# Order of two VectorE operations in the fifth step of each FFN chunk, in a macaron block on one core

## The reference, cut to what matters

```python
gate = jnp.einsum('bsd,hd->bsh', x, wg)      # x: layer norm of the input, 256 -> 768
up = jnp.einsum('bsd,hd->bsh', x, wu)
h = jax.nn.silu(gate) * up
ffn = jnp.einsum('bsh,dh->bsd', h, wd)       # 768 -> 256
x = x + 0.5 * ffn(layernorm(x))
x = x + attn(layernorm(x))                   # causal, 16 heads
x = x + 0.5 * ffn(layernorm(x))
```

## Time and profile before

| | |
|---|---|
| runs before | 1781.88 to 1790.09 us, median 1786.74 us |
| the profiled execution | 1802.57 us, of which 1800.8 us from the first to the last instruction |
| TensorE busy | 1630.5 us (91%), mean granted clock 0.942 |
| VectorE busy | 1206.3 us (67%) |
| ScalarE busy | 1024.0 us (57%) |
| GpSimd busy | 427.6 us (24%) |

### The profile page before, as it was taken

How to read it: one execution, slowest core, us unless ns; L and a number is a source line. 1 busy time by engine, 2 the same in 40 slices (tenths; PEclk the granted TensorE clock), 3 DMA queues, 4 the chain that set the end, 5 groups by cost and what they waited for, 6 DMA issues and landing times. The chain is left out here.

```text
span 1800.8 us, 37764 instructions
## 1 busy us (share of the span) xinstructions
PE 1630.5 (91%) x12418; PEld 942.9 (52%) x12418; DVE 1206.3 (67%) x2701; ACT 1024.0 (57%) x2032; POOL 427.6 (24%) x656
## 2 busy tenths in 40 slices
PE   5999999459999989989989989989998887999998
PEld 4888888314444334334334334334343236888887
DVE  5565654378888878778878768777877725655553
ACT  4444443137767757657757757757766655434343
POOL 3454544311101101101101011111010003544443
PEclk9999999659999989889989989989999898999999
DMA  7000000400200200100200200200200001101011
GB/s 240 1 0 0 0 0 1 139 13 18 61 14 21 58 14 21 58 14 8 71 14 8 63 19 11 58 20 11 62 22 11 5 1 54 36 23 35 23 35 36
DMA packets 46949, 58.46 MB, mean 32 GB/s; under 512 B 6112, under 2 KB 33504, under 8 KB 46816
## 3 DMA queue, kind: packets, MB, share of 16 engines
q1 hardware_dynamic: 46816, 56.51, 10.2%
HBM read 30.53 MB, written 25.17 MB: 31 GB/s over the span
## 5 line engine op out<-in xcount | busy, mean ns | idle before, releaser
L1045 ACT ACTIVATE at_probs<-at_banks 128x512 f32<-128x512 f32 (+1 forms) x1280 | 635.7, 560 | 350.2 <-PE at_banks L1233 269.2
L1149 DVE TENSOR_REDUCE at_maxima<-at_banks 128x1 f32<-128x512 f32 (+3 forms) x1024 | 532.7, 581 | 162.9 <-PE at_banks L1233 121.2
L1225 PE MATMUL at_banks<-at_q_rows,at_k_rows 30*128 30x512 bf16 (+3 forms) x1536 | 322.2, 343 | 62.8 <-issue 33.3
L1225 PE MATMUL at_banks<-at_k_rows,at_q_rows 27*128 27x512 bf16 (+3 forms) x1536 | 331.5, 348 | 25.7 <-DMA at_q_rows<-q_rows_dram 16.2
L1252 PE MATMUL at_o_ps<-at_probs,at_v_aug 128*32 128x512 f32 (+3 forms) x3072 | 338.3, 530 | 8.7 <-ACT at_probs L1045 5.6
L390 PE MATMUL ffn_gate_up<-ffn_x_hi,ffn_w_hi 128*128 128x512 f32 x768 | 307.5, 400 | 19.5 <-DVE ffn_x_lo L274 11.8
L181 POOL TENSOR_TENSOR ffn_h_lo<-ffn_h_sb,ffn_h_hi 128x512 fp32r<-128x512 f32 x192 | 247.2, 1295 | 261.1 <-ACT ffn_h_hi L210 223.5
L390 PE MATMUL ffn_gate_up<-ffn_x_lo,ffn_w_hi 128*128 128x512 f32 x768 | 304.1, 396 | 0.0
L291 DVE TENSOR_TENSOR ffn_h_sb<-ffn_act_sb,ffn_gate_up 128x512 f32<-128x512 f32 x192 | 131.5, 686 | 237.4 <-PE ffn_gate_up L390 135.2
L217 ACT ACTIVATE ffn_act_sb<-ffn_gate_up 128x512 f32<-128x512 f32 x192 | 115.1, 600 | 308.0 <-PE ffn_gate_up L390 302.7
L1225 PEld LDWEIGHTS at_banks<-at_q_rows,at_k_rows 30*128 30x128 bf16 x1536 | 83.9, 92 | 379.7 <-issue 134.3
(11 more groups left out here) (84 smaller groups left out, 1490.4 us busy)
## 6 DMA issues: line engine op xcount, KB each, us to landing
x<-x_in SPq DMA_DIRECT2D x16, 512.0 KB, 4.6
at_k_rows<-k_rows_dram SPq DMA_DIRECT2D x32, 256.0 KB, 2.8
at_q_rows<-q_rows_dram SPq DMA_DIRECT2D x64, 128.0 KB, 2.1
out<-x SPq DMA_DIRECT2D x16, 512.0 KB, 2.9
q_rows_dram<-at_qk_parts SPq DMA_DIRECT2D x72, 96.0 KB, 2.4
k_rows_dram<-at_qk_parts SPq DMA_DIRECT2D x72, 96.0 KB, 2.4
at_q_rows<-at_max_t SPq DMA_DIRECT2D x256, 3.0 KB
ffn_w_f<-w_gate SPq DMA_DIRECT2D x2, 768.0 KB, 5.2
```

The costliest lines, as they stand in the source:

```text
L1045: nc.scalar.activation(probs[:, (g * NE + u) % PROBS, j, 0:n], banks[:, used[0], 0:n], ACT.Exp).then_inc(exp_done, 1)
L1149: last = nc.vector.tensor_reduce(out, banks[:, used[0], o:o + n], AX_X, ALU.max)
L1225: last = nc.tensor.matmul(banks[:, n, o:o + width], stationary, moving, start=(k == 0), stop=(k == len(pieces) - 1 and not masks))
```

## The change

In step 4 VectorE subtracts the two halves of `x_lo` first and adds the second half of the residual behind them. In step 3 nothing changes.

```diff
--- before.py
+++ after.py
@@ -301,10 +301,10 @@
                 up(m)
                 if m == 0 and not last:
                     ln_gather()
+                if m == 4 and not last:
+                    split_x(c + 1, 1 - p)
                 if m in (3, 4) and not first:
                     residual(c - 1, m - 3)
-                if m == 4 and not last:
-                    split_x(c + 1, 1 - p)
 
         ln_stats(0, 0)
         dve.wait_ge(stats_done, 1)
```

## The result

The changed kernel took 1768.61 us (median of 8 runs, 1761.36 to 1776.30) and the kernel before, in the same sessions, 1788.41 us (8 runs, 1776.65 to 1795.90). The ratio is 0.9893 with a 95% interval of 0.9862 to 0.9925: 13 to 25 us less, 19.8 us by the medians. The forecast was 15.9 us less and 1770.8 us. The profiled execution after is the slowest of the eight (1776.30 us), and the one before, 1802.57 us, is slower than all eight, so times are compared by the medians and the traces only stretch by stretch.

What follows compares the result with a forecast made beforehand. TensorE bounds the FFN stages, stopping for `x_lo` at 28 chunk boundaries; 11.0 + 2.1 + 2.8 = 15.9 us off the median of 1786.74 gives 1770.8 us, range from 5.8 us below that to 1779.0.

Steps and rivals of the forecast that it cites:

- The bound and the stop: FFN stages: TensorE sets the pace; its stop for `x_lo` at chunk boundaries, 0.51 us in ffn1, goes wholly.
- `x_lo` at its new place: VectorE, directly behind `up(4)`: the pair still takes about 1.28 us and is good 0.6 us ahead of TensorE's load.
- The slow restart: TensorE behind each boundary stop: second matmul after 0.33 instead of 0.23 us; 28 x 0.10 = 2.8 us gained.
- The residual and `up(5)`: VectorE, step 4 to 5: the later residual costs nothing and `up(5)` keeps its time, with 0.5 us of cover.
- GpSimd as the next to be late: First `down` of a chunk: `h_lo` holds with 0.24 us of cover; rival that it fails, about 1775 us, chance 0.08.
- The sum: 28 FFN chunk boundaries: 11.0 us in the loop, 2.1 outside it, 2.8 of slow restarts, together 15.9 us.
- the loop edge: FFN loop-head jumps: their delay takes the wait's place at 14 boundaries, 8.0 us left of the gain, 1778.7 us; chance 0.12.
- the clock in attention: Attention stage: TensorE's granted clock falls, 11.6 us more per hundredth, making the kernel slower, about 1795 us; chance 0.05.
- a change of attention by more than some 5 us: Attention stage: its length changing by more than some 5 us was set as a sign that the prediction is wrong.

Runs made afterwards that it cites:

- the last kernel: Changed kernel, attention included, with the last chunk's first `down` waiting for `h_lo` part by part: 1768.33 us (7 runs), ratio 0.9893 to the kernel before.

## Why the prediction was right

The measured 1768.61 us lie 2.2 us below the forecast. That they lie so near is in part luck: the forecast went out from a median of 1786.74 us of three runs, where eight gave 1788.41. By the difference it was 15.9 us against 19.8, of which about 17 belong to the FFN stages.

- **The bound and the stop.** Right. TensorE's order is the same, the stops of rows 4 and 9 are gone, and the forecast's 0.61 us a chunk was 0.62 in ffn1 and 0.63 in ffn2.
- **`x_lo` at its new place.** Right: 1.29 us for the pair, beside ScalarE and GpSimd. The text gave it 0.6 us of cover with the signal counted; measured are 0.80 to the load, 0.67 with the signal. The reason was tested apart: one extra subtraction is free, two are not.
- **The slow restart.** Right as a cost of its own: it vanished with the stop, came back with a stop of 0.30 us, and appeared without any stop when `h_lo` came at the last moment. The rows of the load say why: released late, it goes out with its matmul (142.92 and 142.93) instead of 0.23 us ahead, and costs 0.10 us; with 0.10 us of lead (140.57 and 140.67) it costs 0.01.
- **The residual and `up(5)`.** Right: `up(5)` starts 0.49 us after the step's last matmul starts (141.02 to 141.51), before it was 0.53, and one step later the addition costs nothing either.
- **GpSimd as the next to be late.** Right that it is the nearest and that it holds; the 0.24 us with the signal were measured as 0.23. But the text took the operand load as the deadline, and `x_lo` 0.14 us behind it cost only 0.03 us a chunk. By the matmul's own time the cover is 0.46 us.
- **The sum.** A little low: 15.9 us forecast, 16.9 in the traces of the whole kernel, 17.3 without attention. In the trace before, the 28 stops add up to 13.3 us and the slow restarts to 2.9, 16.2 in all, so the count was 0.3 us low. Of that 0.1 us are the three boundaries a stage outside the loop, taken as the middle of two rows (0.35 us each; in the trace they are 0.39, 0.43 and 0.31 in ffn1 and 0.37, 0.42 and 0.30 in ffn2). The other 0.7 us is spacing of the matmuls that differs by fractions of a percent between the executions, and was not settled.
- **The rivals: the loop edge.** It costs nothing: 0.23 us at each jump. The text said that no row shows a jump by itself; there is one, in the trace before too, with 0.21 to 0.24 us, and the sequencer makes the jump some 3 us before the boundary's first matmul. The rule of the Trainium skill that spoke for the rival (Runtime: NRT & Kernel Launch, Instruction fetch mechanics) is about a target outside the instruction window. The trace agrees with it: the attention loop's jumps move instruction packets and take 3.6 to 4.3 us, and the FFN loop's, during which none moves, are not such a case. So the text applied the rule to the wrong loop. That the attention loop is the longer one (some 1130 matmuls an iteration against 208) fits, but no run here changed a loop's length.
- **The rivals: the clock in attention.** It did move, in the friendly direction, 9.5 us in the profiled execution. The text named a change of attention by more than some 5 us as a sign that the prediction is wrong. That sign came, and it was badly set: attention differs by 18.3 us between the traces of the new order and of the last kernel, and the kernel before scatters as much by itself. The price was 11.6 us for each hundredth of clock, and the three stretches give somewhat less, 27.8 us for the 0.03 from 0.91 to 0.94. Which way it moves is chance as far as these runs show, which is why the kernels without attention were needed to measure 17 us well.

## What to carry to other kernels

On an engine that works in order, look at what stands in front of the instruction that the bounding engine waits for: if that one waits for something nobody needs soon, exchange the two, and count the stop from start to start with the slow restart behind it (0.51 + 0.10 us here, against 0.34 us of idle time in the waits). Then compute what is late next against the new, earlier time, to the matmul's start and not only to its operand load, and check the cover with extra work whose length is read from a trace in which it stands where it will stand: here it was free up to the threshold, and past it cost its lateness and the slow restart. Look at the rows of the sequencer before a jump is blamed. Where a stage without changes scatters more than the gain, leave it out for the measurement.

## What the runs showed of the hardware

- An operand that became good between the time of a matmul's operand load and the matmul's own time delayed almost nothing at first: 0.14 us behind the load cost 0.03 us a chunk (the residual between the halves), 0.23 us cost 0.10 (three additions on GpSimd). After a late release the second matmul started 0.33 us after the first with 512 columns and 0.22 with 256, where an unbroken stream has 0.23 and 0.12.
- After a stop of 3.3 us at a stage's end the next 48 matmuls ran at a granted clock of 1.00 at six stage ends and lower at seven, 5.4 to 5.7 against 7.1 to 8.3 us. The kernel whose stop was split into two of 1.0 to 1.3 us scattered by 0.5 us over four runs, the others by 1.5 to 4.3.
- A jump of TensorE's sequencer to the head of the FFN loop took 0.21 to 0.24 us and cost nothing, with no instruction packet from 80 to 260 us; to the head of the attention loop it took 3.6 to 4.3 us, with instruction packets, and TensorE stood idle for 33.4 us behind five of them.
- Three 128x4 additions on GpSimd took 0.50 us in a row and held back the next operation by 0.45, though one alone has a row of 0.20 us.
